# A graph attention network and an FFN on one core: the FFN's second product as three passes of split values, the atoms' weights through two buffers, and the plans read where they are used

## What is computed

```python
x = x + gnn(layernorm(x), edge_index, W1, ..., W2, ...)   # 8 heads of 128, relu, then 1 head of 768
x = x + ffn(layernorm(x)[None], ...)[0]

def ffn(x, ...):
    cls_tokens, patch_tokens = x[:, :6], x[:, 6:]
    patch_out = gelu(patch_tokens @ fc1_w.T + fc1_b) @ fc2_w.T + fc2_b          # 768 -> 384 -> 768
    gate_logits = einsum('bnd,nrd->bnr', l2norm(cls_tokens), l2norm(gate_pair)) + balance_bias
    route_probs = softmax(gate_logits)
    hid_all = gelu(einsum('bnd,ahd->bnah', cls_tokens, atom_in_w) + atom_in_b)  # five atoms
    route_candidates = einsum('bnrh,nrdh->bnrd', picked_hidden, atom_out_w[dst]) + atom_out_b[dst]
    cls_out = the candidate of the likelier route, times its probability
    return concatenate([cls_out, patch_out])
```

## Time and profile before

| | |
|---|---|
| median of 3 runs | 733.5 us (733.22 to 735.07) |
| the profiled execution | 733.38 us, span 731.6 us |
| PE busy | 717.2 us, 98% of the span |
| PE weight load busy | 655.3 us, 90% |
| DVE busy | 519.4 us, 71% |
| ACT busy | 390.7 us, 53% |
| POOL busy | 105.2 us, 14% |
| granted clock of PE | full in all slices |

### The profile page before, as it was taken

How to read it: one execution, slowest core, us unless ns; L and a number is a source line. 1 busy time by engine, 2 the same in 40 slices (tenths; PEclk the granted TensorE clock), 3 DMA queues, 4 the chain that set the end, 5 groups by cost and what they waited for, 6 DMA issues and landing times.

```text
span 731.6 us, 13048 instructions
## 1 busy us (share of the span) xinstructions
PE 717.2 (98%) x4607; PEld 655.3 (90%) x4607; DVE 519.4 (71%) x940; ACT 390.7 (53%) x749; POOL 105.2 (14%) x95
## 2 busy tenths in 40 slices
PE   8999999999999999999999999999999999999998
PEld 6798999789899999999999999999999898978965
DVE  5899888699999999999999452336567542717141
ACT  4565573388698889888988931122221413322100
POOL 2566120000000000000000000000223330222211
PEclk9999999999999999999999999999999999999999
DMA  8636655659111121302230020001882544225011
GB/s 284 210 98 195 183 153 168 180 168 336 39 71 36 71 49 57 105 14 91 64 143 0 0 57 1 1 0 36 247 266 85 178 139 153 89 63 176 22 37 49
DMA packets 39664, 78.92 MB, mean 108 GB/s; under 512 B 4073, under 2 KB 25391, under 8 KB 38720
## 3 DMA queue, kind: packets, MB, share of 16 engines
q1 hardware_dynamic: 33932, 60.53, 27.3%
q10 hardware_dynamic: 4500, 13.82, 5.6%
q0 software_dynamic: 1184, 3.92, 1.8%
HBM read 62.97 MB, written 15.29 MB: 107 GB/s over the span
## 4 chain that ended last, share of the span: by engine, by line
PE 94%; DMA 3%; ACT 1%; issue 1%; DVE 1%; ACTq 0%; SPq 0%; POOL 0%; POOLq 0%; DVEq 0%
PE bank L1245 23%; PE bank L1387 15%; PE bank L1224 12%; PE bank L1316 12%; PE bank L1117 11%; PE bank L1463 5%; PE bank L1483 5%; DMA w1n_sb<-in_W 3%; PE bank L1034 3%; PE bank L1368 1%; PE bank L1261 1%; PE bank L1435 1%; PE bank L1049 1%; PE bank L1451 1%; PE bank L1036 1%; PE bank L1498 1%
## 5 line engine op out<-in xcount | busy, mean ns | idle before, releaser
L1245 PE MATMUL bank<-PT,h1s 125*128 125x250 f32 x800 | 175.8, 374 | 0.0
L1245 PEld LDWEIGHTS bank<-PT,h1s 125*128 125x128 f32 x800 | 148.7, 190 | 15.6
L1829 DVE SCALAR_TENSOR_TENSOR L<-asb,nadh 125x1250 f32<-125x1250 f32 x80 | 118.0, 1517 | 3.1 <-PE bank L1224 1.3
L828 ACT COPY PT<-bank 125x500 f32<-125x500 f32 x200 | 99.7, 597 | 37.8 <-PE bank L1224 37.8
L1837 DVE CUSTOM_DVE_ANT_0 L<-L,LC 125x1250 f32<-125x1250 f32 x80 | 113.4, 1455 | 0.0
L815 ACT ACTIVATE L<-L,nm 125x1250 f32<-125x1250 f32 x80 | 107.8, 1371 | 0.0
L1224 PEld LDWEIGHTS bank<-ident,L 125*125 125x125 f32 x800 | 93.3, 189 | 3.9 <-ACT L L815 1.5
L1224 PE MATMUL bank<-ident,L 125*125 125x125 f32 x800 | 94.6, 273 | 0.7 <-ACT L L815 0.7
L2010 DVE TENSOR_TENSOR x2f<-bank,x2f 125x384 f32<-125x384 f32 x20 | 10.3, 552 | 63.5 <-PE bank L1483 63.5
L1646 DVE TENSOR_TENSOR hotr<-iota,r 125x1500 f16<-125x1500 f16 x50 | 46.6, 931 | 10.0 <-PE bank L1036 5.8
L1387 PE MATMUL bank<-h_hi,PT_hi 125*125 125x384 f32 x200 | 42.1, 353 | 0.0
(11 more groups left out here) (247 smaller groups left out, 1214.8 us busy)
## 6 DMA issues: line engine op xcount, KB each, us to landing
asb<-src_logit_rows SPq DMA_DIRECT2D x7, 1250.0 KB, 5.8
atom_w<-in_atom_inT SPq DMA_DIRECT2D x5, 1152.0 KB, 13.0
atom_w<-in_atom_outT SPq DMA_DIRECT2D x5, 1152.0 KB, 9.9
log_count_scratch<-LCw SPq DMA_DIRECT2D x10, 546.9 KB
LC<-log_count_scratch SPq DMA_DIRECT2D x10, 546.9 KB
LCt<-log_count_scratch SPq DMA_DIRECT2D x10, 546.9 KB
h_scratch<-h1st ACTq DMA_DIRECT2D x10, 448.0 KB
h1s<-h_scratch SPq DMA_DIRECT2D x7, 560.0 KB
```

Source lines behind the costliest of these rows:

```text
L828: act.copy(PT[(k - lag) % 2][:, 2 * b:2 * b + 2, :], bank[turned_bank(first, k - lag, b)][0:NP, 0:2 * GW].rearrange("p (s n) -> p s n", s= ...
L1245: mm = pe.matmul(bank[2 + (k - lag) % 2][:, 0:GW], h1s[q][:, s, :], PT[(k - lag) % 2][:, s, :], start=(s == 0), stop=(s == NT - 1))
L1829: dve.scalar_tensor_tensor(L[r][:, :], asb[q][0:NP, 1, :], nadh[q][:, t:t + 1], asb[q][0:NP, 0, :], ALU.add, ALU.max).then_inc(stt_done, 1)
```

## The change

1. **ffn_down in three passes.** fc2's weights are split once into fc2_hi (ACT, `fc2_upper`) and fc2_lo (DVE, `fc2_lower`). Of each group's gT the upper part gT_hi is cast by ACT right after the gelus, and DVE makes the lower part (`hidden_lower`). A column half is nine split matmuls, in an order in which the pieces of the third gelu come late. fc2_lo takes fc2_sb's memory, gT_lo takes gT's, and gT_hi takes that of `scr`. For this last one ACT waits for `gate_step` 5 before the first group's copies.
2. **Two buffers for the atoms' weights.** The third buffer's memory holds fc2_hi. load_atom(s) waits for load s-2's buffer. The units are taken four at a time, the second four after half (i, 1, 0), and turn_units comes after ffn_down(i-1, 0). In round 3 the candidates of atoms 0 and 1 stand where all three stood, and those of atom 2 after ffn_down(2, 1). SP's queue has the loads at other places.
3. **Plans read at the counts.** `count_plan` stands directly before each count_edges (for tile 8 one piece of products before, for tile 9 before the turn), no longer ahead of the turn.

```diff
+        fc2_hi = sb("fc2_hi", [128, KF, D], F32R, two_ctx)
+        gT_lo = sb("gT_lo", [128, KF, GW], F32R, two_ctx)
...
+        fc2_lo = sb("fc2_lo", [128, KF, D], F32R, p4)
...
+        whole = ExitStack()
+        scr = sb("scr", [NCLS, D], F32, whole)
+        whole.close()
+        gT_hi = sb("gT_hi", [128, KF, 256], F32R, p4)
...
             def load_atom(s):
-                if s >= 3:
-                    sp.wait_ge(atom_used, s - 2)
+                if s >= 2:
+                    sp.wait_ge(atom_used, s - 1)
...
+            def fc2_upper():
+                act.wait_ge(ffn_in, 32)
+                act.wait_ge(h2b_done, NT)
+                for m in range(KF):
+                    act.copy(fc2_hi[:, m, :], fc2_sb[:, m, :]).then_inc(gelu_done, 2)
             def units_out(part):
+                act.wait_ge(atom_used, (2, NATOM)[part])
...
             evac_5(1)
+            fc2_upper()
+            act.wait_ge(gate_step, 5)
             ffn_5(0, tokens=True)
...
+            ORDER = [("hh", 0), ("hh", 1), ("hl", 0), ("hl", 1), ("hh", 2), ("hl", 2), ("lh", 0), ("lh", 1), ("lh", 2)]
             def ffn_down(i, j):
...
-                    for m in range(KF):
-                        mm = pe.matmul(bank[down_bank(i, j) + b][0:NP, 0:HALF], gT[:, m, j * NP:(j + 1) * NP],
-                                       fc2_sb[:, m, b * HALF:(b + 1) * HALF], start=(m == 0), stop=(m == KF - 1))
+                    for n, (term, m) in enumerate(ORDER):
+                        rows, weights = DOWN[term]
+                        mm = pe.matmul(bank[down_bank(i, j) + b][0:NP, 0:HALF], rows[:, m, j * NP:(j + 1) * NP],
+                                       weights[:, m, b * HALF:(b + 1) * HALF], start=(n == 0), stop=(n == len(ORDER) - 1))
...
                 if i < 3:
+                    atom_units(i - 1, 4)
+                ffn_down(i - 1, 0)
+                if i < 3:
                     turn_units(i - 1)
-                ffn_down(i - 1, 0)
-                if i >= 3:
-                    candidates(4 - i)
+                elif i == 3:
+                    candidates(1, some=(0, 1))
+                else:
+                    candidates(0)
                 half_5(i, 1, 1)
                 ffn_down(i - 1, 1)
+                if i == 3:
+                    candidates(1, some=(2,))
...
             gate_logits()
             logits_5(4)
+            fc2_lower()
             norm_5(1, 0)
+            hidden_lower(0)
             out_5(0, 0)
```

More of the change, by code:

```diff
@@ L293, in gnn_ffn_kernel @@
         h2_lo = sb("h2_lo", [NP, NT, D], F32R, p4)
-        scr = sb("scr", [NCLS, D], F32, p4)
+        whole = ExitStack()
+        scr = sb("scr", [NCLS, D], F32, whole)
+        whole.close()
+        gT_hi = sb("gT_hi", [128, KF, 256], F32R, p4)
         as2c = [sb(f"as2c{p}", [NP, 1], F32, p4) for p in range(2)]
@@ L523, in _ @@
             lc_load(3)
-            for s in range(3):
+            for s in range(2):
                 load_atom(s)
@@ L531, in _ @@
                     sp.dma_start(bo[n:n + 1, r, :], atom_outb[rows[n]:rows[n] + 1, :]).then_inc(bo_in, 16)
+            load_atom(2)
             lc_load(5)
-            for s in range(3, 5):
-                load_atom(s)
+            load_atom(3)
             lc_load(6)
@@ L538, in _ @@
             lc_load(7)
-            for s in range(5, 8):
+            for s in range(4, 7):
                 load_atom(s)
@@ L544, in _ @@
             lc_load(9)
+            for s in range(7, 9):
+                load_atom(s)
             out_store(2, 0)
-            for s in range(8, 10):
-                load_atom(s)
+            load_atom(9)
             out_store(2, 1)
@@ L1125, in products @@
                         if count and (part, b) == count[0]:
-                            count_edges(*count[1:])
+                            count_edges(count[1], count_plan(count[1]))
+                        if count and count[0] == (part, None) and b == 7:
+                            plan_ahead = count_plan(count[1])
                     if t < FUSED and part == 0 and whole:
@@ L1185, in _ @@
                 if i == 5:
[L1186 to L1193, removed]
+                    count_edges(5, count_plan(5))
                 turn(i + 1)
-                products(i, count=count)
+                products(i, count=inside.get(i))
+            plan_9 = count_plan(NT - 1)
             turn(NT - 1)
@@ L2001, in norm_5, with fc2_lower, hidden_lower @@
                                   ALU.subtract, ALU.mult).then_inc(y_ready, 1)
+            def fc2_lower():
+                dve.wait_ge(gelu_done, 6)
+                for m in range(KF):
+                    s = dve.tensor_tensor(fc2_lo[:, m, :], fc2_sb[:, m, :], fc2_hi[:, m, :].bitcast(F32), ALU.subtract)
+                s.then_inc(ffn_lo_done, 1)
+            def hidden_lower(i):
+                dve.wait_ge(gelu_done, 6 * (i + 1) + 6)
+                dve.tensor_tensor(gT_lo[:, :, :], gT[:, :, :], gT_hi[:, :, 0:GW].bitcast(F32), ALU.subtract
+                                  ).then_inc(ffn_lo_done, 1)
             def out_5(i, j):
@@ L2102, in _ @@
             norm_5(2, 0)
+            hidden_lower(1)
             out_5(1, 0)
@@ L2112, in _ @@
             norm_5(3, 0)
+            hidden_lower(2)
             out_5(2, 0)
@@ L2120, in _ @@
             norm_5(4, 0)
+            hidden_lower(3)
             out_5(3, 0)
@@ L2124, in _ @@
             out_5(3, 1)
+            hidden_lower(4)
             for j in range(2):
```

79 lines of the change are left out of this document (44 added, 35 removed).

## The result

The changed kernel takes **747.1 us** (median of 4 runs, 745.47 to 748.07); the kernel before took 733.4 beside it (4 runs, 733.09 to 735.07). The ratio is 1.0176, 95% interval 1.0159 to 1.0193: slower by 1.8%, as forecast in sign, but 7.3 us above the 739.8 of the forecast and 1.6 above the end of its range. The profiled execution took 746.74, its span 744.9.

What follows compares the result with a forecast made beforehand. The prediction took the matrix engine (PE) as the bound, busy 717.2 of 731.6 us. Its terms, -5.0 - 3.0 + 5.3 + 1.0 + 7.5 + 0.6 + 0 = +6.4, took 733.4 to 739.8 us, range 736.5 to 745.5.

Steps and rivals of the forecast that it cites:

- Part 3: Before the atoms' first units: ACT waits for the gate's scratch, so PE waits for the yT and tokT copies, +5.3 us.
- Part 5: Last group's turns: PE waits for DVE's chain behind the last candidates, +7.5 us, and a later lower_5(4), +0.6.
- Part 2: First phase: plans read at the counts bring back idle at turns, products and tile 8's count, -3.0 us.
- Part 1: ffn_down in three passes: 0.71 us saved per call, seven of ten calls counting, -5.0 us.
- Part 4: Atoms' weights in two buffers: loads stay hidden, but three more pieces start, +1.0 us.
- rival C: Last phase: load 7 of the atoms' weights lands late and PE waits 1 to 3.5 us more, 742; chance 0.07.
- Part 6: The rest: extra casts and lower parts hidden; in the tail two short gaps against two shorter calls, 0 us.
- B: First phase: plan reads are dear at the nine counts, +4 in place of -3, 746.8 us (half: 743.3); chance 0.13.
- D: Both sizes small: long gate operations shrink (-3.1) and passes save more (-1.8), 734.9 us, no change; chance 0.06.
- E: First phase's turns: each read blocks PE for its whole length, moved reads worth 9.5 to 23.4 us, 726.3; chance 0.04.

Runs made afterwards that it cites:

- run 3: The changed kernel with the edits of run 1 and run 2 together: 730.2 us, ratio 0.9945 to the kernel before.
- run 1: The changed kernel with scr in memory of its own, so that ACT's wait for the fifth gate operation goes: 736.5 us, ratio 1.0035 to the kernel before.
- run 2: The changed kernel with add_route(1) moved on DVE behind logits_5(9) and norm_5(3,1): 737.3 us, ratio 1.0048 to the kernel before.
- run 5: The kernel before with one line added, ACT waiting for the fifth gate operation ahead of the first yT copy: 741.6 us, ratio 1.0102.
- run 6: The changed kernel with both waits kept and PE given 42 and 60 throw-away transposes in them: 741.3 us, ratio 1.0094 to the kernel before.
- run 12: The changed kernel measured again, unaltered: 744.5 us, ratio 1.0142 to the kernel before.
- run 4: The kernel before with only the plans' reads moved to the counts: 732.3 us, ratio 0.9975.
- run 10: The kernel of run 9 with the plan of tile 4 read ahead of its turn again: 729.0 us, ratio 0.9930 to the kernel before.
- run 7: The kernel of run 3 with ffn_down in full precision as before, without DVE's subtractions: 735.0 us, ratio 1.0011 to the kernel before.
- run 8: The kernel of run 3 with the last third of the candidates ahead of round 3's second ffn_down: 730.1 us, ratio 0.9947 to the kernel before.
- run 9: The kernel of run 8 with add_route(1) put ahead of norm_5(3,1): 729.5 us, ratio 0.9931 to the kernel before.
- run 11: The kernel of run 10 with only the four copies ahead of norm_5(3,1), the addition behind lower_5(4): 728.3 us, ratio 0.9919 to the kernel before.

## Why the prediction was right and wrong

**The sign and the mechanism were right.** Two bare waits outweigh the shorter passes; with both mended the same change is faster than before (run 3).

**Part 3** had the gate wait at 5.3, and 5.32 was measured, twice. The step that failed is the sentence "Above, nothing: no load is in this chain": a wait of PE costs more than its length. The term should have been 5.3 plus 1.5 to 2.7, as runs 1, 2, 5, 6 and 12 show.

**Part 5** had 7.5 and 0.6: measured 7.56 and 0.64 (run 6). "Nothing in this chain can shrink; its bounds are 7.2 and 8.5" failed in the same way: 1.3 to 1.8 more for the clock. The earlier trace rows show the clock at the top throughout, but in a kernel whose PE never waits longer than 1.54 us; I took the clock of a kernel without long waits for that of one with two. No rival of the prediction spoke of the clock either.

**Part 2** was mis-sized: -3.0 forecast, -1.9 measured (run 4, and every profile since). The step that failed is "All this together is 4.5 us that can come back": of its three pieces the 3.2 of idle came back, the 0.9 of late weight loads and the 0.4 of tile 8's count did not. The new cost came out near its size by luck (1.5 forecast, 1.3 measured): the forecast had four long reads at 0.3 to 0.5 each, and no read was long. What there is, is 0.85 at tile 4 and 0.12 and 0.32 at tiles 3 and 7. The premise that failed is "a read comes behind 24 to 42 long products": tile 4's comes behind twelve, and giving it more lead brought its 0.85 back (run 10). The bounds (-4.5 to +4) held the sum.

**Parts 1 and 4** were right: -5.0 and +1.0 forecast, together -3.95 in run 3; run 7 gives 4.8 (medians) to 5.2 (trace) for the passes alone. The working by four passes to three, which the prediction had beside the row, would give 6.8. No transfer of atoms' weights was late, not even with load 7 wanted 3.2 us earlier (run 8), so rival C is out.

**Part 6** was 0, measured -0.3. The profile marks the two gaps with 0.30 and 0.36, but that is not what they cost. The 36 split matmuls of the last two calls run from 733.97 to 741.84, 7.87 us, where the two calls before took 7.90 (720.57 to 728.47). The two shorter calls should save 1.4 and save 0.03, so the gaps cost about 1.4, as the forecast's 1.3 had it; the -0.3 lies mostly ahead of these calls.

**Rivals.** B is out by run 4 (that its 746.8 lies next to the measured 747.1 is a coincidence), C by run 8, D by the sizes of both waits, E because the moved reads bring 1.9 in place of 9.5 or more.

**The sum.** Forecast +6.4, profile +13.3. Of the 6.9 between them, 4.5 is the clock (2.67 + 1.83), 1.1 the reads, 1.45 the late start by chance, 0.1 the waits' sizes and -0.3 the tail. In the second measurement, without the late start and with shorter slow stretches, the time was 744.5, inside the range. That is luck too: 744.5 - 739.8 = 4.7 holds 2.8 of clock that the forecast had at nothing, and 1.1 of reads; the 0.8 left isn't assigned (the medians of the kernel before alone differ by 1.5, 733.4 to 734.9).

## What to carry to other kernels

A stall of the tensor engine is priced as its length plus what the work behind it loses at the lower clock, here 1.3 to 2.7 us more for a wait of 5 to 8. If such a wait must stay, throw-away transposes in it are worth having (741.3 for 744.5 to 747.1), but a buffer that is not shared, or one instruction moved on the waiting engine, is worth more. And when an operation is moved out of a wait's chain, look at what was behind it: run 9 only moved the wait, run 11 split the operation and kept what PE wants ahead.

## What was not expected of the hardware

The granted clock fell from 1.00 to 0.50 in the course of every wait of 5 to 8 us. In the waits of 0.2 to 1.7 us it stayed at 1.00, with one exception: in run 4 it fell just after the wait of 1.72 us that ended at 28.28, and the 64 matmuls behind took 4.45 us for 2.79. It may not be rare: of the 66 executions of the kernel before that were timed beside the experiments, 12 have a mean granted clock of 0.997 or 0.998 over the whole run and a median of 736.1 us; the other 54, at 0.999 or 1.000, have 734.1. In which stretch those twelve were slow isn't known. So a short wait isn't safe, and why the clock falls in one execution and not in the next wasn't found. How long it then stays low differs between executions of the same program: it is at 0.50 until the stretch 562 to 563 in the first profile and until 558 to 559 in the second, each time with PE busy from the moment its wait ended. The Trainium skill (TensorE: Matmul & The Clock Gate, Part 1) says of a kernel's start that the length of its slow stretch varies between runs; these two profiles show the same behind a wait in mid-kernel.

A count's loop is sensitive to when its plan is read, and one (tile 8) takes 3.46 us wherever that is; why isn't settled. That the low clock is all there is behind the slow records rests on the records themselves, which take 1.8 to 2.0 times as long while the clock is at half (2.79 for 1.52, 5.24 for 2.83, 2.88 for 1.47), and on run 6; what triggers the return wasn't tried. The best kernel of the study, run 11, is 728.3 us against 734.9 beside it, with its interval wholly below 1 by 0.6 to 1.1%. Three of the eleven executions beside it are of the kind at 0.998, so the 6.6 us between the medians is somewhat more than the kernel itself is worth.
